# Attention of a two-layer network: row maxima in a ring of three one-bank buffers, and TensorE's order from a list schedule

## What is computed

```python
# x: [2, 2048, 256], w_qkv: [256, 768]; 16 heads of 16 numbers
qkv = x @ w_qkv                      # x is normalised first
q, k, v = jnp.split(qkv, 3, axis=-1) # to heads: [B, H, T, D]
q = _apply_rope(q, cos, sin)
k = _apply_rope(k, cos, sin)
att = jnp.einsum('bhtd,bhsd->bhts', q, k) * scale
att = jnp.where(causal_mask[None, None], -jnp.inf, att)
att = jax.nn.softmax(att, axis=-1)
o = jnp.einsum('bhts,bhsd->bhtd', att, v)
return o.transpose(0, 2, 1, 3).reshape(B, T, C) @ w_out
```

## Time and profile before

| what | value |
|---|---|
| time, median of 3 runs | 1667.48 us (1660.11 to 1671.02) |
| the profiled execution's own time | 1663.91 us |
| its span in the profile | 1662.0 us |
| TensorE, VectorE, ScalarE busy, whole span | 79%, 77%, 59% |
| attention, first row-maximum matmul to last product with v | 148.7 to 1019.1 us |

### The profile page before, as it was taken

The page is one execution under the profiler, slowest core; times in us unless marked ns, Lnnn a source line. Parts: engine busy times, 40 slices in busy tenths (PEclk is TensorE's granted clock), DMA queues, the critical chain, the costliest instruction groups (busy, mean ns, idle before and its releaser), DMA issues. The chain is left out here.

```text
span 1662.0 us, 27637 instructions
## 1 busy us (share of the span) xinstructions
PE 1316.7 (79%) x9558; PEld 588.4 (35%) x9558; DVE 1271.5 (77%) x1880; ACT 987.9 (59%) x1292; POOL 319.4 (19%) x574
## 2 busy tenths in 40 slices
PE   4783788888888888888888987888727876679987
PEld 2442222222222222222222222566523343358754
DVE  6984887988779787798897951478758999575668
ACT  3541355777768777677786886556417646236642
POOL 2210000110101101011010110322100047600365
PEclk9896577999889998899998998899967988789999
DMA  7875302140321403204032022656644134576767
GB/s 219 277 228 149 65 8 41 18 91 9 76 41 19 92 7 75 42 17 91 10 74 42 8 44 61 182 178 199 201 162 138 61 127 155 182 229 203 236 194 237
DMA packets 159723, 186.24 MB, mean 112 GB/s; under 512 B 19556, under 2 KB 135652, under 8 KB 158564
## 3 DMA queue, kind: packets, MB, share of 16 engines
q1 hardware_dynamic: 153448, 167.78, 35.9%
q0 software_dynamic: 6144, 16.79, 3.1%
HBM read 100.88 MB, written 83.36 MB: 111 GB/s over the span
## 5 line engine op out<-in xcount | busy, mean ns | idle before, releaser
L1270 ACT ACTIVATE att_prob<-att_score,late_score_scale 128x1024 f32<-128x1024 f32 (+3 forms) x640 | 594.7, 988 | 271.4 <-PE att_score L1359 269.3
L1241 DVE TENSOR_REDUCE att_m_part<-att_mx 128x2 f32<-128x1024 f32 (+3 forms) x408 | 473.3, 1160 | 97.5 <-PE att_mx L1308 43.6
L1343 PE MATMUL att_pv<-att_prob,early_v 128*32 128x512 f32 (+3 forms) x2560 | 324.5, 581 | 0.5 <-POOL att_prob L1206 0.2
L1302 PE MATMUL att_mx<-early_kop,early_qop 48*128 48x512 f16 (+3 forms) x944 | 181.1, 367 | 118.0 <-DVE att_m_part L1241 106.2
L1359 PE MATMUL att_score<-early_qop,early_kop 50*128 50x512 f16 (+3 forms) x1280 | 261.0, 369 | 12.4 <-ACT att_prob L1270 5.9
L1206 POOL TENSOR_SCALAR_AFFINE_SELECT att_prob<-att_prob 128x256 f32<-128x256 f32 x256 | 103.1, 407 | 767.6 <-ACT att_prob L1270 767.4
L1241 DVE TENSOR_REDUCE att_m_part<-att_mx_one 128x1 f32<-128x384 f32 (+1 forms) x336 | 220.9, 657 | 37.4 <-PE att_mx_one L1302 32.1
L1359 PEld LDWEIGHTS att_score<-early_qop,early_kop 50*128 50x128 f16 x1280 | 69.5, 95 | 293.5 <-ACT att_prob L1270 188.7
L1302 PE MATMUL att_mx_one<-early_kop,early_qop 48*128 48x384 f16 (+1 forms) x336 | 134.1, 399 | 19.7 <-DVE att_m_part L1241 15.9
L2108 PE MATMUL rwkv_prod<-rwkv_xm,late_mixT 128*128 128x512 f32 x192 | 100.1, 677 | 29.1 <-DVE rwkv_xm L1978 16.6
L1302 PEld LDWEIGHTS att_mx<-early_kop,early_qop 48*128 48x128 f16 x944 | 51.7, 97 | 190.9 <-DVE att_m_part L1241 165.9
(11 more groups left out here) (259 smaller groups left out, 1901.2 us busy)
## 6 DMA issues: line engine op xcount, KB each, us to landing
moe_xt<-rows SPq DMA_DIRECT2D x46, 256.0 KB, 3.3
results<-moe_y SPq DMA_DIRECT2D x46, 256.0 KB, 2.6
qk<-qkv_parts SPq DMA_DIRECT2D x32, 256.0 KB, 3.6
va<-qkv_v SPq DMA_DIRECT2D x8, 1024.0 KB, 6.5
early_v<-va SPq DMA_DIRECT2D x8, 1024.0 KB, 5.2
routing_xp<-parts SPq DMA_DIRECT2D x32, 256.0 KB, 3.7
rows<-att_zeros SPq DMA_DIRECT2D x8, 864.0 KB, 6.2
early_kop<-qk SPq DMA_DIRECT2D x48, 128.0 KB, 4.5
```

The costliest lines, as they stand in the source:

```text
L1241: nc.vector.tensor_reduce(cells[:, sides[0]:sides[-1] + 1, some], bank.rearrange("p a (h w) -> p a h w", w=w), AX.X, ALU.max).then_inc(m_f ...
L1270: nc.scalar.activation(prob[:, r % (PROBS * HP), :, n0:], score[:, r % 2, :, n0:], ACT.Exp, scale=late_weights.score_scale[:, 0:1])\
L1302: op = nc.tensor.matmul(bank[a][:, n * w:(n + 1) * w], qop[rows, slot, t, hp, i * P:(i + 1) * P], kop[rows, slot, hp, c * GT:c * GT + w], ...
L1343: op = nc.tensor.matmul(pv[at, n0:], v[:, slot, j, at], prob[:, (st * HP + h // 2) % (PROBS * HP), h % 2, n0:], start=(j == 0), stop=(j == ...
```

## The change

1. **One-bank ring.** `mx_one` goes; `mx` has three banks, entry k uses bank k % 3. Every entry is a single: `chunks` gives each item once for a = 0 and once for a = 1. An iteration has 144 entries in place of 93, all with the same columns in sum.
2. **Order of TensorE and ScalarE.** `spread_entries` goes. `matrix_order` puts entries, score pairs and products in one list: it keeps an estimate of when each engine is through and always takes the kind that could start first, an entry when they are even. `BEHIND` goes too; ScalarE's copy of a finished block follows the same list.
3. **Unrolled.** The loops of VectorE and GpSimd are written out.
4. **Loads of q.** `load_q` takes several blocks at a time, one transfer for each head pair: 12 instead of 24 in an iteration, and 12 instead of 18 at the end of the projections. All of a slot's q now signal `first_in`.
5. **Projections.** From group 1 on, `turn` of the new group stands ahead of `heads` on TensorE, `high` ahead of the parts on ScalarE, and `low` ahead of `products` on VectorE.

```diff
-            for t in range(1, att_in.QB):
-                att_in.load_q(sp, qk_d, 0, 0, 0, t, att_in.second_in if t == 1 else att_in.rest_in[0])
+            att_in.load_q(sp, qk_d, 0, 0, 0, slice(1, att_in.QB), att_in.second_in)
...
+                early = mid and mid[0] == 0
+                if new and not early:
+                    low(*new)
                 for p in range(QK):
                     if mid:
                         products(*mid, p)
                         rotated(*mid, p)
-                if new:
+                if new and early:
                     low(*new)
...
-        items = [whole[0], rest[0], whole[1]] + rest[1:]
...
+        return [("max", t, *item, (a,)) for item in whole + rest for a in range(2)]
...
+    def banks_of(k):
+        return (k % BANKS,)
...
+    def matrix_order():
+        hand, back, mask, row, copy = 250, 120, 420, 6500, 580
+        turn = {"max": 0, "score": 1, "value": 2}
...
+            if n < total["max"]:
+                it, e = entries[n]
+                need = [bank_end[bank] for bank in banks_of(n)] + ([found[it, e[1]]] if e[0] == "turn" else [])
+                ready.append((max(need) + back, "max"))
+            n = done["score"]
+            if n < total["score"]:
+                it, st, hp = score_at[n]
+                if (it, steps[st][0]) in rows and n // HP < done["value"] + PROBS:
+                    need = [rows[it, steps[st][0]]] + [end + back for end in exp_end[n - 2:n - 1] if n >= 2]
+                    ready.append((max(need), "score"))
+            n = done["value"]
+            if (n + 1) * HP <= done["score"]:
+                need = prob_end[n * HP:(n + 1) * HP] + (out_end[-1:] if steps[n % NS][1] == 0 else [])
+                ready.append((max(need) + back, "value"))
+            when, kind = min((max(pe, when), turn[kind], kind) for when, kind in ready)[::2]
...
-        mx = s.ps("mx", [P, 2, GT])
-        mx_one = s.ps("mx_one", [P, 1, GT])
+        mx = s.ps("mx", [P, BANKS, GT])
...
-            with eng.Fori(0, NIT // 2 - 1) as i:
...
+            for k, (it, e) in enumerate(entries):
+                entry(k, it, e)
```

More of the change, by code:

```diff
@@ L889, in step @@
                 ahead, new, mid, old = at
+                early = mid and mid[0] == 0
                 if old:
                     values(*old)
+                if new and not early:
+                    high(*new)
                 if mid and mid[0] >= late_from:
@@ L1069, in attention_phase @@
-    spots, start_spots = spread_entries(), spread_entries(True)
+    entries = [(0, e) for e in early if e != ("turn", LATE)]
+    for it in range(NIT):
+        entries += [(it, e) for e in late]
+        entries += [(it, e) if e == ("turn", LATE) else (it + 1, e) for e in early if it + 1 < NIT or e == ("turn", LATE)]
+    place = {entry: k for k, entry in enumerate(entries)}
+    def banks_of(k):
+        return (k % BANKS,)
+    used, before = {}, []
+    for k in range(len(entries)):
+        before.append(max((used.get(bank, -1) for bank in banks_of(k)), default=-1))
+        used.update({bank: k for bank in banks_of(k)})
@@ L1070, in attention_phase @@
+    order = matrix_order()
     with ExitStack() as ctx:
@@ L1210, in _ @@
             nc.gpsimd.memset(zeros[:, :], 0.0).then_inc(zeros_set, 1)
-            schedule(pool, iteration, lambda: None)
+            for it in range(NIT):
+                iteration(it)
         @block.vector
@@ L1284, in _, with entry @@
             pv_done.open(pe)
-            def entry(it, slot, e, freed):
-                if freed is not None:
-                    pe.wait_ge(m_found, freed)
+            def entry(k):
+                it, e = entries[k]
+                slot = it % 2
+                if it > 0 and e == chunks(0)[0]:
+                    pe.wait_ge(first_in[slot], (it // 2 + 1) * FIRST)
+                    pe.wait_ge(rest_in[slot], (it // 2 + 1) * REST)
+                if it == 0 and e == chunks(1)[0]:
+                    pe.wait_ge(second_in, att_in.SECOND)
+                if it == 0 and e == chunks(2)[0]:
+                    pe.wait_ge(rest_in[0], REST)
+                if before[k] >= 0:
+                    pe.wait_ge(m_found, before[k] + 1)
+                banks = [mx[:, bank] for bank in banks_of(k)]
                 if e[0] == "turn":
@@ L1379, in _, with scores @@
-            first()
-            for it in range(NIT):
-                iteration(it, it % 2, it // 2, it + 1 < NIT, spots if it else start_spots)
-            for st in range(NS - BEHIND, NS):
-                products(NIT - 1, st)
+            def scores(it, st, hp):
+                slot, r = it % 2, st * HP + hp
+                t, j = steps[st]
+                n0 = max(0, j - TG * t) * P
+                if r == 0:
+                    pe.wait_ge(first_in[slot], (it // 2 + 1) * FIRST)
+                    pe.wait_ge(rest_in[slot], (it // 2 + 1) * REST)
+                    pe.wait_ge(lift_in, 32)
+                if j == 0 and hp == 0:
+                    pe.wait_ge(m_in[t], it * (M_SENT) + 2 * (M_SENT))
+                pe.wait_ge(exp_done.sem, exp_done.freed(it * NP + r, 2))
+                for hh in range(2):
+                    rows = slice(HALF * hh, HALF * hh + ROWS + MROWS)
+                    op = nc.tensor.matmul(score[:, r % 2, hh, n0:], kop[rows, slot, hp, j * P:(j + 1) * P],
+                                          qop[rows, slot, t, hp, n0:], start=True, stop=True)
+                op.then_inc(score_done.sem, 1)
@@ L1384, in attention_phase @@
+            pe.wait_ge(cells_set, 1)
+            pe.wait_ge(att_in.ident_in, 16)
+            pe.wait_ge(att_in.mask_in, 16)
+            pe.wait_ge(first_in[0], FIRST)
+            for kind, *at in order:
+                if kind == "max":
+                    entry(*at)
+                elif kind == "score":
+                    scores(*at)
+                else:
+                    products(*at)
         return s.signals
```

272 lines of the change are left out of this document (104 added, 168 removed).

## The result

| | before | after |
|---|---|---|
| time, median | 1665.06 us (1660.11 to 1671.02) | 1591.92 us (1589.24 to 1595.33) |
| ratio, 95% interval | 1 | 0.9565 (0.9543 to 0.9587) |
| span of the profiled execution | 1662.0 us | 1586.0 us |
| VectorE's stretch in the attention | 149.4 to 977.1: 828 us | 145.0 to 907.1: 762 us |
| from there to the last copy of the attention | 43 us | 38 us |

The change makes the kernel 73 us faster, 4.35%. The two profiled spans differ by 76 us: 66 in VectorE's stretch, 5 behind it and 4.4 ahead of it; the rest of the network, 641 us, is 1.3 us shorter.

A forecast was written before the change was run, and what follows sets the result against it. The prediction saw TensorE, VectorE and ScalarE waiting in a circle, and VectorE as bound after the change. Terms -66, -7, -4 and -3.5 gave -80 on 1662.0, span 1582, forecast 1588 us; range of 8 in 10: 1560 to 1640.

The forecast's parts named there:

- VectorE's stretch, -66: VectorE's time in the attention: 702 us of work plus 60 of gaps, 762 us against 828.
- The loops inside it: VectorE's loop turns in the attention: 2.95 us of issue each, three times at most, 9 us, counted within the -66.
- The ring ends the gaps whatever the order: VectorE's gaps in the attention come from one buffer to fall back on; the ring ends them whatever the order.
- The price of a single: Reductions on VectorE: two singles cost 1.22 us, 0.08 more than a pair, so 33 us more work.
- Behind the stretch, -7: From the last m_row to the attention's last copy: 36 us against 43, bounds -11 and 0.
- Projections and loads, -4 and -3.5: Before the attention: half of VectorE's 8.8 us wait saved (-4), 12 load issues instead of 18 (-3.5).
- One stretch of low clock an iteration: Attention: one lower-clock stretch stays in each iteration, where eight entries stand in a row behind t = 2's last product.
- Rival 1: Attention: the clock and TensorE take the gain back, one or two more low-clock stretches an iteration, about 1625 us; chance 0.17.
- Rival 2: Attention: the ring buys nothing, the fixed order is off and gaps stay at 18 us an iteration, 1686 us; chance 0.08.
- Rival 3: Attention: the ring works, but the fixed order leaves gaps of 10 to 14 us an iteration, about 1640 us; chance 0.13.
- Rival 4: Attention: better than forecast, VectorE nearly without gaps, 20 us in all, 1550 us; chance 0.07.
- TensorE's 77 us an iteration: TensorE's work in an attention iteration after the change: some 77 us, close under VectorE's 88.

The follow-up runs named there:

- e1: The kernel before with only the loops of VectorE and GpSimd written out: 1644.94 us beside 1661.74, ratio 0.9908.
- e3: The changed kernel with its listed order replaced by the old one that spreads entries over the score pairs, ring kept: 1626.62 us, ratio 0.9805.
- e4: The changed kernel with the old pair and single buffers in place of the ring, listed order planned for them: 1686.83 us, ratio 1.0152.
- e6: The changed kernel with two banks in the ring in place of three, order kept entry by entry: 1860.76 us, ratio 1.1173.
- e2: The kernel before with only the reordered projections and the q loads of several blocks at a time: 1661.88 us, ratio 0.9996.
- e11: The changed kernel with two planner constants changed, row's way 5.0 us instead of 6.5 and exponentials counted 9% longer: 1615.95 us on a slower chip, ratio 0.9437.
- e10: The kernel of e11 with each reduction reading only 448 of 512 columns: 1545.09 us, ratio 0.9288.
- e9: The changed kernel with an unread maximum over 16 columns behind each reduction on VectorE: 1691.49 us, beside 1641.15 for the changed kernel on the same chip.
- e5: The changed kernel with an unread fill of one cell behind each of the 1152 reductions on VectorE: 1596.68 us, ratio 0.9593.
- e8: The changed kernel with the matmuls of entries standing five or more in a row issued twice into the same bank: 1596.48 us, ratio 0.9581.

## Why the prediction was right, point by point

**VectorE's stretch, -66: right in sum (762 forecast, 762 measured), from errors that cancel, which is luck.** The stretch before, the stretch now, and the seven iterations in it between sends (length, VectorE busy, clock, DMA):

```profile
149.40:977.10 827.70, 684.62 (x842) 0.91 0.20 42
145.00:907.10 762.10, 699.03 (x1249) 0.93 0.25 46
204.13:871.39 667.26, 611.55 (x1093) 0.94 0.26 47
```

After the change VectorE is busy 699 us and idle 63, and I had 702 and 60. But before it the same reading gives 685 and 143, and I had 669 and 159. So the work grew by 14 us and not by 33, and the gaps fell by 80 and not by 99. I had taken the overlap with a neighbour off every reduction, also off those that follow a wait, like the one at 868.06 in the earlier trace rows, which overlaps nothing; part of a single's price had been paid in the gaps. The turns I had at 35 us; their three lines are busy 8.9, 8.7 and 7.0 us, 25 in all. Nor were the gaps where I put them. I took 25 us for the first iteration and 5 for each of the other seven. Measured, the seven have 55.7 us, 8 each and 21 more in all; what lies outside them (145.0 to 204.1 and 871.4 to 907.1) has 7.4 us, 18 less than I took. The claim that a cold TensorE is slow in any order failed: in 160 to 200 us the clock is 0.75 where it was 0.54, and VectorE has 35.2 busy where it had 31.3.

**The loops inside it: mis-sized.** I counted 2.95 us a turn, 9 in all for three; the trace has two such gaps. e1 measured 15 to 17, 7 in the iteration behind each of the two, the rest in the first iteration, where it isn't tied to the loop. The row showed the gap; it did not show that the circle of waits passes it on and the clock falls behind it.

**"The ring ends the gaps whatever the order": this step failed.** With the loops at 15 to 17, the ring alone brings 18 us (e3 beside e1), and the order on the ring 35 to 40. e4 shows that the order on the old buffers costs 42 us. The reason I gave for the gap, one buffer to fall back on, was right as far as it went: with two banks the same order loses 269 us (e6). But how much of a buffer's depth is used is the order's doing.

**The price of a single: right where reductions stand one behind another.** The starts are 0.61 us apart, so two singles cost 0.08 us more than a pair. The page "VectorE: DVE Perf Modes", section "The TRN2 errata", of the Trainium skill has 120 cycles (0.125 us) as the fixed part for a source in PSUM. The trace has 0.08 us of it in the starts, and the measurement decides.

**Behind the stretch, -7: measured -5.** From the last m_row (907.1) to the last copy (945.3) are 38 us. The first scores of t = 3, before and now:

```profile
986.31 0.61 PE L1359 MATMUL att_score<-early_qop,early_kop 50*128 50x512 f16 x4
911.31 0.61 PE L1349 MATMUL att_score<-early_qop,early_kop 50*128 50x512 f16 x4
```

They came 9.2 us behind the last m_row and now come 4.2 us behind it, and the block takes 33.7 and 34.0 us from there. So all of the 5 us lie ahead of the block. The 28.7 us that I carried over were a misreading: 991.27 in the earlier trace rows is the fifth exponential of t = 3, not the first. Too short a block and too long a way of the row (7 us) nearly cancelled.

**Projections and loads, -4 and -3.5: measured -4.4 together, and not seen in the time when alone.** VectorE's idle time before `by_cos` fell from 8.8 to 3.4 us, but `low` now waits 6.6 us for `high` in place of 2.7, the very cost I had named with +5: 1.5 us are left of the 4. The loads took 7.75 us in place of 10.60. This is 0.65 us an issue of 48 rows against 0.59 for 32, so -2.85 and not -3.5. In the phase:

```profile
L828 DVE TENSOR_TENSOR qkv_by_cos<-qkv_qk_ps,qkv_cos 128x1024 f32<-128x1024 f32 x16 | 19.5, 1218 | 3.4 <-PE qkv_qk_ps L102 3.3
...
L352 DVE TENSOR_TENSOR qkv_ln_lo<-qkv_turned,qkv_ln_hi 128x1024 f16<-128x1024 f32 x8 | 9.8, 1223 | 6.6 <-ACT qkv_ln_hi L347 6.6
```

Attention begins 4.4 us earlier in the changed kernel and 2.5 earlier in e2; I had said near 141, it is 145.0.

**One stretch of low clock an iteration: right,** in the place named, behind the last product of t = 2. It costs some 3 us of VectorE each time (7.76 or 6.47 busy of 10), and e11 shows that an order without it has nearly none of those gaps.

**What would show it.** 1152 reductions, 0.61 us apart, ScalarE waiting 188 us: as said. VectorE's idle before the reductions was to be under 60 in sum and is 60.0, at the edge. The clock is below 1.00 in more places than the one I named, and attention begins at 145.0 and not near 141. The iteration of 95.3 lies just above 91 to 95.

**The rivals.** Rival 1 didn't come: behind the first iteration (0.57 at 240 to 250 us) there is no second stretch near the lower level in an iteration, only windows of 0.83 to 0.86 in three of the seven. The page "TensorE: Matmul & The Clock Gate", section "A second HAM failure mode", of the Trainium skill describes the swing of the clock through idle pieces between banks. The traces show such a swing in e4 (0.50) and e6 (0.81 in the mean), where the ring is missing or shallower, and once an iteration after. Rival 2's condition, an order that is off makes TensorE stop at entries, is what e4 does with pairs: its 1687 is the number that I gave for the rival, by another way, so the agreement is chance. Rival 3's gaps of 10 to 14 us an iteration didn't come either: they are 8. Rival 4's 1550 isn't reached even by e11.

**TensorE's 77 us an iteration: not what the trace shows.** In 200 to 900 us of the changed kernel TensorE is busy 668.9 us and VectorE 642.6. At a clock of 0.98 (e10) TensorE still shows 85 us an iteration. The ends of matmuls are modelled, so this doesn't make TensorE the bound, but with e9 (two thirds of the added work reach the time) and e10 (a third of the removed work comes off) VectorE is the larger part of the path and not all of it.

## What to carry to other kernels

Judge buffers and the order of a fixed program together: here the ring gave 18 us, the order without the ring cost 42, and both gave 53 to 57. Where several engines wait in a circle, a gap seen in one row costs more than its length (2.95 us became 7), and a wait that leaves TensorE with only work that needs a slower engine's buffers also costs clock; plan the order so that every engine has work through the longest latency, even by telling the planner that an engine is slower than it is (tried here with one value). Before using added work as a probe, look whether it really moves the starts of the work beside it.

## What the runs showed of the hardware that I had not expected

- The turn of a loop on VectorE: 2.95 and 2.89 us of issue in the kernel before, and 7 us in the iteration behind each (e1), with the granted clock at 0.66 behind it.
- A fill of one cell (0.06 us) between two reductions of 512 columns leaves their starts 0.61 us apart (e5); a maximum over 16 columns, whose duration is 0.16 us, moves them by 0.065 (e9).
- One bank fewer in the ring, with the same order, costs 269 us (e6), 34.5 us an iteration.
- Doubling the matmuls of a run that waits for VectorE's banks did not keep the clock at its upper level (e8).
- Two chips differ outside the attention and hardly in it: the changed kernel took 1641 us on one chip and 1592 on another, with 764 and 762 us of VectorE's stretch in their profiles; behind the attention's end (948.8 and 945.3 us) lie 689 and 641 us.
